# Two cross-attention layers on one core: where eight tiles, an output product and a split stand between the score maxima

## What is computed

```python
# layer 0, for each batch (text = ctx[:77], ip = ctx[77:])
q, k, v = x @ Wq.T, text @ Wk.T, text @ Wv.T          # and k_ip, v_ip from ip
out = softmax(q k / 4) v + softmax(q k_ip / 4) v_ip   # per head
x1 = out @ Wo.T + bo + x
# layer 1 (text = ctx[:371], ip = ctx[371:])
probs = softmax(q k / 4)
sem = l2norm(probs @ text) . l2norm(ip)
out = probs v + (softmax(q k_ip / 4 + sem / 2) * mask) v_ip
y = out @ W_out + b_out + x1
```

## Time and profile before

| | |
|---|---|
| median of three runs | 2507.5 us |
| the profiled execution | 2511.88 us |
| its span, first to last instruction | 2510.1 us |
| mean granted TensorE clock | 0.995 |
| PE busy | 2439.8 us (97%) |
| PEld busy | 2121.7 us (85%) |
| DVE, ACT, POOL busy | 1582.6, 1262.6, 902.9 us |

### The profile page before, as it was taken

The page is one execution under the profiler, slowest core; times in us unless marked ns, Lnnn a source line. Parts: engine busy times, 40 slices in busy tenths (PEclk is TensorE's granted clock), DMA queues, the critical chain, the costliest instruction groups (busy, mean ns, idle before and its releaser), DMA issues.

```text
span 2510.1 us, 64311 instructions
## 1 busy us (share of the span) xinstructions
PE 2439.8 (97%) x26372; PEld 2121.7 (85%) x26372; DVE 1582.6 (63%) x2961; ACT 1262.6 (50%) x2315; POOL 902.9 (36%) x1382
## 2 busy tenths in 40 slices
PE   7899999999999999999999999999999999999998
PEld 6788888888888888888888888888888888888876
DVE  4455667666667665667655667556677556676655
ACT  3355545455454555554555454555554554454543
POOL 3233333333333333333333333333333333333323
PEclk9999999999999999999999999999999999999999
DMA  9965556664556755457655476645566645566620
GB/s 216 138 97 88 97 92 99 105 110 80 87 90 103 118 86 89 87 95 113 105 82 88 88 106 107 104 82 93 95 98 105 104 76 91 92 95 107 93 33 14
DMA packets 371690, 241.45 MB, mean 96 GB/s; under 512 B 131947, under 2 KB 365243, under 8 KB 371388
## 3 DMA queue, kind: packets, MB, share of 16 engines
q1 hardware_dynamic: 371398, 237.35, 57.6%
HBM read 171.35 MB, written 64.59 MB: 94 GB/s over the span
## 4 chain that ended last, share of the span: by engine, by line
PE 79%; DVE 9%; POOL 5%; DMA 2%; issue 2%; ACT 1%; SPq 1%; DVEq 0%; POOLq 0%; ACTq 0%
PE ST L839 7%; PE R L783 5%; PE R L784 5%; PE R L770 5%; PE R L905 5%; PE PN L878 5%; PE R L715 4%; POOL w L1474 4%; PE R L786 4%; PE R L716 4%; PE R L963 3%; DVE w L999 3%; DVE m L1082 3%; PE R L718 3%; PE PN L923 3%; PE ST L821 2%
## 5 line engine op out<-in xcount | busy, mean ns | idle before, releaser
L1474 POOL TENSOR_TENSOR w<-w 128x448 f32<-128x448 f32 (+1 forms) x256 | 330.9, 1292 | 381.1 <-DVE w L996 360.1
L999 DVE SCALAR_TENSOR_TENSOR w<-p,pr 128x1344 f32<-128x1344 f32 x160 | 297.5, 1860 | 163.8 <-ACT pr L1339 151.5
L1311 ACT ACTIVATE p<-ST 128x1344 f32<-128x1344 f32 x260 | 335.8, 1291 | 95.8 <-PE ST L842 90.8
L905 PE MATMUL R<-pr,Gh 128*128 128x448 f32 (+1 forms) x960 | 365.9, 381 | 0.0
L996 DVE TENSOR_TENSOR rem<-R,kst 128x298 f32<-128x298 f32 (+2 forms) x180 | 89.5, 497 | 425.7 <-ACT kst L1190 425.7
L1387 POOL TENSOR_TENSOR kst<-rem,kst 128x298 bf16<-128x298 f32 (+2 forms) x180 | 148.0, 822 | 522.5 <-ACT kst L1190 286.1
L996 DVE TENSOR_TENSOR w<-R,w 128x448 f32<-128x448 f32 (+1 forms) x480 | 281.5, 620 | 68.7 <-PE R L910 58.8
L783 PE MATMUL R<-wvh,ch 128*128 128x320 f32 (+3 forms) x896 | 302.9, 338 | 0.0
L784 PE MATMUL R<-wvh,cl 128*128 128x320 f32 (+3 forms) x896 | 277.1, 309 | 0.0
L839 PE MATMUL ST<-Qs,Ks 100*128 100x112 bf16 (+1 forms) x3520 | 228.7, 214 | 8.3 <-ACT p L1311 3.2
L839 PEld LDWEIGHTS ST<-Qs,Ks 100*128 100x128 bf16 (+1 forms) x3520 | 187.9, 98 | 46.8 <-issue 13.6
(11 more groups left out here) (231 smaller groups left out, 5848.1 us busy)
## 6 DMA issues: line engine op xcount, KB each, us to landing
Ks<-k_split SPq DMA_DIRECT2D x384, 140.6 KB, 5.8
Ks<-k_split SPq DMA_DIRECT2D x384, 93.8 KB, 8.2
w<-in_ctxT SPq DMA_DIRECT2D x31, 750.0 KB, 10.0
k_split<-kst SPq DMA_DIRECT2D x64, 281.2 KB, 3.8
k_split<-kst SPq DMA_DIRECT2D x64, 223.5 KB, 3.0
Qs<-q_split SPq DMA_DIRECT2D x64, 210.0 KB, 9.0
q_split<-qst SPq DMA_DIRECT2D x128, 84.0 KB, 2.3
Qs<-q_split SPq DMA_DIRECT2D x64, 140.0 KB, 9.2
```

The lines of the kernel that those rows point to most:

```text
L905: e.matmul(r[0:nj, 0:QW], Gh[0:ROWS[u], q:q + nj], x[0:ROWS[u], QW * u:QW * u + QW], start=u == 0, stop=False)
L999: return e.scalar_tensor_tensor(out=to, in0=x, scalar=s, in1=y, op0=op0, op1=op1)
L1311: e.activation(to.rearrange("p (u q) -> p u q", u=3), st, ACT.Exp).then_inc(p_whole, 1)
L1474: e.tensor_tensor(first, first, w2[n % 2][0:ROWS[j], QW * j:QW * j + QW], ALU.add).then_inc(ns_added, 1)
```

## The change

It concerns passes with 0 < b < 31 for the maxima, and 1 < b < 32 for the transpose of layer 1's maxima.

```diff
         def among0(g):
-            take(rows1, 1)
+            if g or not 1 < b < B:
+                take(rows1, 1)
...
             if count[0] > 9:
-                take(rows0, 1)
-            if count[0] in ((1, 2, 3, 4, 6, 7, 9, 10) if b + 1 < B else (1, 2, 3, 4, 5, 7)):
+                take(rows0, 2 if 0 < b < B - 1 else 1)
+            if count[0] in ((1, 2, 3, 4, 6, 7, 9, 11) if b + 1 < B else (1, 2, 3, 4, 5, 7)):
                 take(last, 1)
-            if count[0] in ((2, 3, 4, 6, 8, 12, 14, 16) if 0 < b < B - 1 else (2, 4, 6, 8, 11, 12, 14, 16)):
+            if count[0] in ((2, 3, 4, 6, 8, 10, 13, 15) if 0 < b < B - 1 else (2, 4, 6, 8, 11, 12, 14, 16)):
                 take(pieces, 1)
```

## The result

The changed kernel took 2464.05 us (median of four runs, 2463.16 to 2470.82) against 2507.78 for the kernel before on the same chip: a ratio of 0.983, interval 0.981 to 0.984. The direction and the places were right; the size was not.

A forecast was written before the change was run, and what follows sets the result against it. PE, busy 97%, was taken to lose time only at steps 10 to 16. The walk's 0.73 plus 0.07 for overlap made 0.80 us a pass, 24 us over 30 passes: 2483.5 us, range 2473 to 2500.

The forecast's parts named there:

- the walk: Stage-by-stage timing of PE in the new order from m_T: s0 comes at 888.04 instead of 888.77, 0.73 us a pass.
- the price of m_T: Transpose ahead of o_mm: 0.52 us start to start less the idle mark of 0.26 taken as 0.26 of PE time.
- The walk's 1.05 for g2: g2 on PE: start to W13's start, less W13's idle mark of 0.50, taken as 1.05 us.
- The 0.07 added for g2's overlap: g2 behind m_T: about half of a possible further gain of 0 to 0.13 us a pass, added to 0.73.
- Its PE time is the same in both places: m_T' moved from behind s0 to behind s1: s0 to s1 shrinks from 2.59 to 2.33 us, gain counted as nothing.
- The new wait at W15: PE at W15, wanted at 885.22 and free at 885.48 because DVE's reads queue behind its add: 0.26 us.
- all three waits gone: Fast end of the range, 2473 us: PE's waits at o_mm, W13 and N14 all vanish, 1.10 us a pass by starts.
- the 70 us of the prediction: PE busy 97% of the span: an order that only moves work can win at most the 70 us PE waits.
- DVE did not take the bound: Rival, W9 to s0: DVE almost without gaps, W15's wait grows, gain only 0.1 to 0.4 us a pass, say 2500; chance 0.13.
- the waits did not move to s1 to s3: Rival: waits only move to the next layer's groups, for instance bound by ACT's exponentials; 2507 us, chance 0.08.
- The staging tile: Slower rival: k01's write behind m_split' on SP lands late and holds up ACT; 2525 us at 6 us landing, chance 0.07.
- holds up nothing: m_split ahead of g2 on POOL and of the output on SP: ready before g2's copies, so no cost.

The follow-up runs named there:

- g2 early: Kernel before, with g2 and the context's split moved behind step 10, and layer 0's maxima split ahead of them: 2552.6 us, ratio 1.019.
- o_mm alone moved: Kernel before, with only the output product moved behind step 11 in passes 1 to 30: 2521.9 us, ratio 1.005.
- the spare products: Kernel before, with spare matmuls put between m_T and o_mm: two products 2506.14 us against 2506.82, four products 2524.7 against 2506.1.
- the two with one part undone: Changed kernel with m_T' left behind s0: 2490.4 us; changed kernel with the last two value tiles back behind steps 14 and 16: 2488.4 us.

## Why the prediction was wrong in size

- **Where PE waits: right.** Steps 10 to 16 were the place, and the marks ahead of o_mm, W13 and N14 are gone, with s0 to s1 at 2.30 (2.33 in the walk). W13 no longer waits because o_mm, 1.62 us, now stands between W11 and W13, where g2, 0.89 us, stood. With neither between them W13 waits 1.26 (g2 early), with both it does not wait (o_mm alone moved).
- **The step that failed: a wait was taken for its mark, and the rest of the interval for work.** The largest such term is the price of m_T. I subtracted the mark of 0.26 from 0.52 us and took the rest, 0.26, for the transpose, and carried that into the new order. I had written two paragraphs earlier that marks understate a wait because ends are modelled, and applied it to N14 only. From start to start the transpose takes 0.03 ahead of g2, and the wait at o_mm was 0.46 to 0.49: the spare products show it. This term is 0.23 us a pass. (Its whole price is nearer 0.10, since g2 no longer overlaps the narrow step: N10's start to g2's last matmul is 1.08 us, 863.19 to 864.27; from N12 to it 0.98 in the trace with o_mm alone moved.)
- **The same error in g2: close by luck.** The walk's 1.05 for g2 held 0.16 of W13's wait, and 1.00 was measured; but that holds the new wait of 0.17 at W11, which the walk did not have. The 0.07 added for g2's overlap came as 0.05.
- **"Its PE time is the same in both places" and no wait elsewhere: wrong.** s0 to s1 fell as foreseen, but s1 to s2 did not grow by 0.26: it went from 2.83 to 2.84. In this pass and 14 others s2 waits for the exponential in both orders, and m_T' disappears in that wait, which I had named and priced at nothing; in the other passes m_T' costs 0.05 (2.67 to 2.72). And k00 had waited for the bank of v01, which I had not seen although I cited w4's wait of 3.47 us and noted that k00's bank changes. I checked the new bank and not the old one. From s0 to s2 the walk kept 5.42 us and 5.14 were measured: 0.28.
- **The new wait at W15: a third of its size.** 0.26 in the walk, 0.08 measured (869.64 - 869.24 less the 0.32 of a narrow step). The walk freed ST 4.83 us behind o_mm's start; DVE's chain took 4.52 to the copy's end (865.07 to 869.59), since the add starts 1.82 behind o_mm rather than 1.88 and takes 0.40 of DVE rather than 0.48, and PE follows 0.05 rather than 0.14 behind. Together with small differences of o_mm, g2, W11 and v02 this is 0.22, and 0.73 + 0.23 + 0.28 + 0.22 = 1.46 is what this pass lost.
- **The same sum by waits, means of a pass.** Gone are 0.46 at o_mm, 0.66 at W13, 0.34 at N14, 0.14 at k00, and 0.08 of the price of m_T' (0.11 less 0.03). New are 0.17 at W11 and 0.08 at W15. That is 1.43, what a pass lost. The terms come from several traces, so the last hundredths are not to be trusted.
- **The cautious bound was no bound.** The fast end of the range was "all three waits gone", 1.10 us a pass, by the waits that I knew of. They came to 1.46, and the fourth to 0.14.
- **What hangs on the Trainium skill** (Perfetto Trace Analysis, Identifying the Most-Contended Engine: matmul busy time is a poor measure, since matmuls are pipelined): the traces agree that it is a poor measure. PE's busy time fell by 18.9 us without a matmul less; a mean clock of 0.997 instead of 0.995 explains some 5 of them, by estimate, and the parts of the waits that no mark shows, 0.68 us a pass before and 0.24 after, explain 13. That section does not speak of waits, though: to trust starts instead was my own step, and the one that I did not carry through. Nor is the idle share of the busy line, the 70 us of the prediction, a bound on what waits.
- **The rivals.** DVE did not take the bound and the waits did not move to s1 to s3. The staging tile was nearer than its chance: ACT's copies into kst waited for a write of keys 4 times before, for 5.4 us in all, and 10 times after, for 16.5, the longest 3.3:
```profile
ACT kst L1191 <- DMA k_split<-kst: 16.5, 10, 3.3
```
No time of PE grew with it: from s2 round to the next m_T a pass takes 60.34 us after and 60.35 before. So it cost nothing here; how near it is to costing something stays open, since I did not run a kernel that separates it.
- **m_split "holds up nothing": right in its place, and silent on why it must be there.** Left behind g2 and the subtractions it turned the gain of 43.7 us into a loss of 64 (2573.6 against 2510.0).

## What to carry to other kernels

Price a stage on a pipelined engine from its start to the next stage's start, in a place where nothing waits, and take a wait as what is left of the interval; the idle marks here were too small by 0.16 to 0.20 us each, because the record of the matmul ahead covers part of the wait. When a list of stages is reordered, write down for every changed slot who was waiting for it in the old order too, since a wait that just ends in time leaves no mark. In this kernel the tiles between steps that another engine must read did best, of the orders tried, where no three steps stand in a row, and what a DMA must deliver ahead of the long operations on the engine that prepares it.

## What the runs showed of the hardware that I had not expected

One wait of TensorE of 1.26 us in a stretch that was otherwise busy was, in 18 of 30 passes, followed by a stretch at a granted clock of 0.50 (1.2 GHz), and one of 2.48 us likewise in 16 of 29. The wait of 0.5 us in every pass before was not, nor were those of 0.6 to 0.8 in the kernel with o_mm alone moved and in the two with one part undone, whose mean clocks were 0.995 to 0.997 against 0.986 with g2 early. So the wait of 1.26 us cost more than itself: the passes without the lower clock were 0.61 us longer than before, those with it 1.98.
